# Where SyncE issues the gathered weights in each step of a streaming residual kernel

## What is computed

```
x = x + einsum('bct,bcd->bdt', x, W0[cond0[b]])                      # 200 matrices of 128x128
x = x + einsum('bct,bcd->bdt', x, W1[cond1[b]]) + bias[cond1[b]]     # 8 matrices, 8 biases
```

## Time and profile before

| | |
|---|---|
| median of 3 runs | 347.73 us (347.19 to 347.92) |
| the profiled execution, its own time | 348.84 us |
| span of the profiled execution | 347.1 us |
| TensorE matmul busy | 266.8 us, 77% |
| VectorE, ScalarE, GpSimd busy | 36%, 28%, 19% |
| moved by the transfers | 140.80 MB, mean 406 GB/s |
| mean granted TensorE clock | 0.961 of full speed |

### The profile page before, as it was taken

One profiled execution on the slowest core, in us unless ns is written; L12 is line 12 of the kernel. 1 busy time (PEld: TensorE's weight loads), 2 busy tenths in 40 slices (PEclk: granted clock), 3 DMA queues, 4 the chain that ended last, 5 costly groups with the idle time before them and its releaser, 6 DMA issues.

```text
span 347.1 us, 5157 instructions
## 1 busy us (share of the span) xinstructions
PE 266.8 (77%) x774; PEld 129.5 (37%) x774; DVE 126.3 (36%) x202; ACT 96.9 (28%) x135; POOL 65.3 (19%) x249
## 2 busy tenths in 40 slices
PE   1799991986798896979877779777679877778980
PEld 1344450442344442434433334433334433333430
DVE  3254541333334242433433344333334333334440
ACT  1133350221333133332232232422242222323230
POOL 2400222112221112221122212122221212221000
PEclk9999997899989898998999999999999999999996
DMA  7999969999999999999999999999999999999994
GB/s 306 410 409 393 378 248 351 424 418 397 417 431 415 433 423 427 417 416 427 432 425 427 427 423 432 421 436 423 419 431 425 432 430 426 423 421 440 419 405 171
DMA packets 24058, 140.80 MB, mean 406 GB/s; under 512 B 2673, under 2 KB 14322, under 8 KB 15474
## 3 DMA queue, kind: packets, MB, share of 16 engines
q1 hardware_dynamic: 23760, 140.20, 97.9%
q10 hardware_dynamic: 290, 0.53, 0.4%
HBM read 76.03 MB, written 67.11 MB: 412 GB/s over the span
## 4 chain that ended last, share of the span: by engine, by line
DMA 56%; SPq 27%; issue 9%; PE 5%; ACT 0%
DMA out<-xy 47%; SPq L127 10%; DMA xy<-x 9%; SPq L122 7%; PE y_ps L306 5%; SPq L128 4%; SPq L142 3%; SPq L145 2%; ACT xy L402 0%; PE m_ps L287 0%; SPq L159 0%; SPq L148 0%; SPq L153 0%; SPq L163 0%; SPq L154 0%
## 5 line engine op out<-in xcount | busy, mean ns | idle before, releaser
L306 PE MATMUL y_ps<-xy,m_sb 128*128 128x512 f32 x512 | 245.5, 616 | 61.3 <-DMA xy<-x 60.3
L306 PEld LDWEIGHTS y_ps<-xy,m_sb 128*128 128x128 f32 x512 | 92.9, 196 | 164.9 <-issue 164.9
L402 ACT ACTIVATE xy<-y_ps,j_pick 128x512 f32<-128x512 f32 x128 | 87.9, 687 | 233.1 <-PE y_ps L306 233.1
L378 DVE TENSOR_SCALAR xy<-y_ps,j_pick 128x512 f32<-128x512 f32 x128 | 96.1, 751 | 156.5 <-PE y_ps L306 156.5
L238 POOL COPY w_pick<-w_home 128x128 f32 x112 | 32.8, 293 | 245.4 <-issue 245.4
L287 PEld LDWEIGHTS m_ps<-j_pick,w_pick 128*128 128x128 f32 x224 | 35.4, 199 | 28.7 <-issue 28.7
L370 DVE TENSOR_TENSOR m_sb<-m_ps,j_pick 128x256 f32<-128x256 f32 x64 | 27.1, 424 | 45.2 <-PE m_ps L287 44.6
L287 PE MATMUL m_ps<-j_pick,w_pick 128*128 128x128 f32 x224 | 35.1, 281 | 0.0
L240 POOL COPY j_pick<-j_all 128x129 f32 x112 | 33.0, 295 | 0.1
L402 ACT ACT_TABLE_LOAD x7 | 9.0, 1283 | 7.9 <-POOL j_pick L252 7.8
L287 PE MATMUL m_ps<-j_pick,w_home 128*128 128x128 f32 x32 | 5.5, 297 | 6.7 <-DMA w_home<-w_t 6.7
(11 more groups left out here) (16 smaller groups left out, 2.8 us busy)
## 6 DMA issues: line engine op xcount, KB each, us to landing
xy<-x SPq DMA_DIRECT2D x30, 2048.0 KB, 15.1
out<-xy SPq DMA_DIRECT2D x29, 2048.0 KB, 13.4
w_home<-w_t SPq DMA_DIRECT2D x128, 64.0 KB
out<-xy SPq DMA_DIRECT2D x5, 1024.0 KB, 6.8
xy<-x SPq DMA_DIRECT2D x3, 1024.0 KB, 7.8
xy<-x SPq DMA_DIRECT2D x4, 256.0 KB, 12.6
j_all<-w_bias SPq DMA_DIRECT2D x1, 516.0 KB, 3.7
out<-xy SPq DMA_DIRECT2D x2, 256.0 KB, 5.1
```

Source lines behind the costliest of these rows:

```text
L306: nc.tensor.matmul(y_ps[:, b % YB, h, :], m_sb[:, s, k, :], xy[:, s, k, half(h)], start=True, stop=True).then_inc(y_ready, 1)
L378: nc.vector.tensor_scalar(xy[:, s, k, half(0)], y_ps[:, b % YB, 0, :], j_pick[:, s, k, D:D + 1], None, ALU.add).then_inc(left_out[b % YB], 1)
L402: nc.scalar.activation(xy[:, s, k, half(1)], y_ps[:, b % YB, 1, :], ACT.Identity, bias=j_pick[:, s, k, D:D + 1]).then_inc(right_out[b % YB ...
```

## The change

The four W0 transfers of a quad are issued one step later: in each step SyncE now issues the store, waits, issues the load of x, and after that the W0 transfers that formerly stood in front of the store. The three last steps and the prologue get the same order: in the prologue the first pairs' stores and the load of quad (1, 0) come ahead of the W0 transfers of (1, 0), and the store of the fourth pair comes between those of (1, 0) and of (1, 1).

```diff
             sp.wait_ge(home_ready, 4)
-            load_w0_of(1, 0)
             for s in range(QUAD + 1):
                 store_pair(0, s)
             load_quad_again(1, 0)
+            load_w0_of(1, 0)
+            store_pair(0, QUAD + 1)
             load_w0_of(1, 1)
-            store_pair(0, QUAD + 1)
             with sp.Fori(1, ROUNDS - 1) as r:
                 for q in range(1, QUADS + 1):
                     now = (r, q) if q < QUADS else (r + 1, 0)
                     after = (r, q + 1) if q + 1 < QUADS else (r + 1, q + 1 - QUADS)
-                    load_w0_of(*after)
                     store_quad(*((r, q - AHEAD) if q >= AHEAD else (r - 1, q - AHEAD + QUADS)))
                     load_quad_again(*now)
+                    load_w0_of(*after)
 
             for q in range(1, QUADS):
-                if q < QUADS - 1:
-                    load_w0_of(ROUNDS - 1, q + 1)
                 store_quad(*((ROUNDS - 1, q - AHEAD) if q >= AHEAD else (ROUNDS - 2, q - AHEAD + QUADS)))
                 if q < QUADS - 1:
                     load_quad_again(ROUNDS - 1, q)
+                    load_w0_of(ROUNDS - 1, q + 1)
```

## The result

The changed kernel takes 349.85 us (median of 7 runs, 348.79 to 351.37) against 347.92 for the kernel before; ratio 1.0051, 95% interval 1.0031 to 1.0070. So it is slower by half a percent, where 0.55% faster was forecast, and above the range. A later set of 12 runs of the same code gave 349.62 (ratio 1.0053, 1.0031 to 1.0074).

The account below looks back on a forecast made before the run. It took the middle as bound by bytes and SyncE as the bound in the prologue's idle stretch; 1.0 + 1.35 - 0.45 = 1.9 us gain, so 346.9 us profiled, 345.8 median, range 344.2 to 348.0.

Parts of the forecast that it names:

- The hole in front: Prologue, 44.6 to 48.3 us: transfer engines idle while SyncE reads registers and issues W0; to shrink by 2.35 less 1.0 us.
- The terms of 1.0 and 1.35 us: Prologue gains: load (1, 0) 1.0 us sooner behind fewer W0 bytes; then 1.35 us from issuing both W0 sets straight-line.
- I cost that at nothing, and the cover is this: Loop: W0 issued one step later costs 0, since picks end in time for TensorE with 3.2 us of slack.
- late W0 in every step: Rival, loop: W0 landing over 7.2 us late delays stores, about 1 us in each of some 26 steps, 372 us; chance 0.05.
- The sum charged 0.45 us: End: the last W0 set's bytes, 2.7 matrices or 0.18 MB, fall after the last big load; a loss of 0.45 us.
- The bound of 0: End: lower limit of the 0.45 us charge, if TensorE's chain to the last move at 337.94 does not see these bytes.

Follow-up runs that it names:

- late_full_hole: The changed kernel with one wait before the loop, for the first round's last results, so the prologue's gain is taken away: 352.59 us, ratio 1.0145.
- late_nogap: The changed loop and end with the prologue of the kernel before, W0 of (1, 0) ahead of the stores: 346.38 us, ratio 0.9958.
- early_nohole: The kernel before with the prologue's W0 set of (1, 1) moved ahead of the wait for the first pairs' stores: 345.56 us, ratio 0.9939.
- early_nohole_2: The kernel before's early W0, loop written as store, load, W0, and the second W0 set ahead of the wait for the first stores: 344.84 us, ratio 0.9919.
- late_no_w0: late_full_hole with every condition false, so no W0 matrix moves after the first 16 and another product is computed: 336.48 us.
- late_later_pick: The changed kernel with GpSimd also waiting, before each quad's first pick, for the first result of the quad before: 348.93 us, ratio 1.0036.
- early_late_end: The kernel before with only the change's last steps, W0 of the last round's third and fourth quads behind the loads: 347.83 us, ratio 1.0001.

## Why the prediction was wrong

**The bound and the prologue: right.** The hole in front was SyncE's, and the middle is bound by the transfers (share 1.01 in both kernels). The terms of 1.0 and 1.35 us came out as 1.0 (load (1, 0) at 33.14) and 1.2 (the rest, to the store at 45.62); that the first agrees so closely is partly luck, since the same prologue gave 32.8 to 33.7 in eight profiles. The lead is worth about its length by the end in the late loop: 3.0 us between late_full_hole and the changed kernel for 2.75 at the front, 3.2 between the changed kernel and late_nogap for 2.1 to 2.4 us of idle engines, 3.0 without W0 for 2.5. In the early loop it was worth less: 2.0 (early_nohole) and 2.5 us (early_nohole_2) for 3.3.

**The loop: this step failed.** The prediction said of W0's later issue "I cost that at nothing, and the cover is this", and then counted whether a product would wait for its pick. That count was right: copies start 1.4 us after TensorE, as computed within half a microsecond, and TensorE waits in the loop for x and hardly for anything else. What failed is the reasoning around it, that a stretch bound by bytes with the same sequence on the queue must take the same time. With the front held as before it takes 4.2 us more to the end of the run (late_full_hole), of which 0.7 is the last set, treated below; so some 3.5 us, 1% of the run, stand where the sum had nothing. Other pairs of kernels put the 4.2 at 2.6 to 4.1. The transfer engines are equally busy and slower. In single profiles of every early kernel with W0's bytes the loop stretch was 254.6 to 258.1 us, in every late one 258.6 to 260.5. The rival "late W0 in every step" had the right place and the wrong mechanism and size: it wanted a delay of over 7.2 us before anything is lost, and 26 us then.

The loss is no even toll on each step. From load (1, 1) to load (3, 0), seven steps, the early kernels with a hole in front need 71.3 to 71.5 us and the late ones with a hole 71.9 to 72.7. From there to load (7, 2), 18 steps with as many matrices in either order, the five early kernels with early copies and the old last steps need 185.7 to 186.4 us and all nine late ones 187.4 to 188.2. These are single profiles.

Of these 3.5 us, 1.5 to 1.7 are shown by medians to come with the moment of GpSimd's copies (two kernels with early W0 and late copies). Their profiles are longer in the 18 later steps (187.4 and 186.8 us) and not in the first seven (70.6 and 71.1). With neither the later matrices' bytes nor late copies next to nothing of the loss is left (late_no_w0). TensorE's clock is excluded to within half a microsecond, the form of the loop to within some 0.6.

**What stays open.** The other 2 us or so, and by what way late copies or young W0 make transfers slower. I have no run that shows the mechanism. Late copies alone do not give the lower rate of the changed kernel at 240 to 300 us: the two kernels with them carry 428 and 429 GB/s there, within the 427 to 430 of all eight early profiles, against 416 to 424 in the nine late ones. late_no_w0 cannot divide the rest, since it takes away the bytes and the late copies together. A run with W0's bytes moved late and the copies early is impossible in this kernel, as a copy cannot come before its matrix; it was not tried with other data. The fall of 0.7 us in late_later_pick is inside the noise.

**The end: mis-sized.** The sum charged 0.45 us because the last set's bytes fall behind the last full load, with as many sets ahead of that load as before. early_late_end does not weigh this. There one set fewer stands ahead of load (7, 2), which goes sooner for it, and the set follows behind: the bytes are the same, and so is the time. The profiles of the others show the term. From load (7, 2) to the end of the span it is 40.8 to 40.9 us in the seven with the old last steps and 41.5 to 41.7 in the ten with the new ones, but 40.0 to 40.1 in both without W0's bytes, of which one has the new steps. So the term is some 0.7 us and part of the 4.2. The sum had taken a mean set of 2.7 matrices; by the input's indices this one moves four, 0.26 MB, an estimated 0.6 us at 424 GB/s. The bound of 0 rested on TensorE's chain, which is over at 337.94 in the kernel before; the transfer engines are still full after it (share 0.98):

```profile
338.00:340.00 2.00, 0.00 (x0) 0.00 (x0) 0.00 (x0) 0.00 (x0) 0.00 (x0) 1.00 0.98 388
```

The last x pieces land 0.3 us too late for TensorE in several profiles with the new last steps, early_late_end among them, whose median does not show it.

**The two sections cited.** Both are of the Trainium skill's page "DMA: Bandwidth & Descriptors". By "Queues, rings and completion order" a transfer's semaphore waits for every earlier write of the same engine. The trace agrees: GpSimd copies the matrices only 1.4 us after the 2 MB load in front of them has released TensorE (115.10 against 113.68). "Anatomy of one DMA" fits its fixed 2.0 us to transfers issued by GpSimd, and the prediction took it over to SyncE's queue, where load (1, 0) would by it have gone at 33.5. The runs cannot tell this from the row's own 1.7 us, which gave 33.2: in eight late profiles with this prologue that load goes at 32.8 to 33.7.

## What to carry to other kernels

When a stretch is bound by transfers, a hole in the queue at the front is worth about its length (here 2.0 to 3.2 us for 2.1 to 3.3 us of idle engines), and the cheapest way to close it is to put issues where the issuing engine would only wait; but follow the queue forward, since issues placed ahead of the first stores only moved the hole. "The same sequence on the queue" does not prove the same time: if the moment at which another engine touches the data moves, let a run decide, and keep operands landing early even where the slack count says that late would do. A change that both closes a hole and moves a landing should be tested with each part alone before its sum is believed: here +4.2 and -2.4 hid behind a ratio of 1.005.

## What the runs showed that I had not expected

- The transfer engines can be equally busy and carry less: share 1.01 at 427 and at 417 GB/s over the same 60 us, the stretch where the two kernels differ most.
- Profiles of one program repeat closely: the changed kernel's two give load (7, 2) at 306.46 and 306.47. Its code with unused register loads gave 305.33, so a microsecond between different programs is not yet a finding.
